# A three-layer interaction network on one core: low parts of four split groups on GpSimd, eleven split groups a phase, one fold for layers 0 and 1

## What is computed

```
def _L0_rec_ref(inputs, w0, w1, w2, b0, b1, b2):
    x0 = inputs
    xk = inputs
    ...
    for idx, (W, b) in enumerate(params):
        z = jnp.einsum('bhd,bkd,hks->bsd', x0, xk, W) + b[None, :, None]
        z = jax.nn.relu(z)
        if idx != n_layers - 1:
            half = z.shape[1] // 2
            xk = z[:, :half, :]
            direct.append(z[:, half:, :])
        else:
            direct.append(z)
    logit = jnp.sum(jnp.concatenate(direct, axis=1), axis=-1)
    return logit
e = jnp.stack([tbl_0[ids[:, 0]], tbl_1[ids[:, 1]], ...], axis=1)
z = _L0_rec_ref(e, L0_rec_w0, L0_rec_w1, L0_rec_w2, L0_rec_b0, L0_rec_b1, L0_rec_b2)
h = jnp.concatenate([z, dense_ctx], axis=1)
h = jnp.maximum(h @ W_top1 + b_top1, 0.0)
h = jnp.maximum(h @ W_top2 + b_top2, 0.0)
y = h @ W_top3
```

## Time and profile before

| | us |
|---|---|
| median of 3 runs | 697.9 (696.61 to 698.32) |
| the profiled execution | 697.3 |
| its span in the profile | 695.5 |
| mean granted TensorE clock | 0.975 of full speed |

### The profile page before, as it was taken

One profiled execution on the slowest core, in us unless ns is written; L12 is line 12 of the kernel. 1 busy time (PEld: TensorE's weight loads), 2 busy tenths in 40 slices (PEclk: granted clock), 3 DMA queues, 4 the chain that ended last, 5 costly groups with the idle time before them and its releaser, 6 DMA issues.

```text
span 695.5 us, 6053 instructions
## 1 busy us (share of the span) xinstructions
PE 640.6 (92%) x1856; PEld 349.2 (50%) x1856; DVE 600.8 (86%) x548; ACT 244.6 (35%) x315; POOL 361.4 (52%) x391
## 2 busy tenths in 40 slices
PE   0159789699999999999999999999999999999998
PEld 0025345355555555555555555555555555555544
DVE  0239679599999999999999999999999999999920
ACT  1112323343433434344334344343433443433312
POOL 6751573864747475766747574747475232232210
PEclk9978899899999999999999999999999999999999
DMA  9679953969493959586776949394958668170100
GB/s 210 125 201 282 304 121 80 321 157 328 82 310 85 283 154 254 180 213 221 164 275 125 318 99 332 76 308 101 285 151 228 204 147 282 65 237 1 62 0 0
DMA packets 126495, 128.14 MB, mean 184 GB/s; under 512 B 61407, under 2 KB 69359, under 8 KB 126464
## 3 DMA queue, kind: packets, MB, share of 16 engines
q1 hardware_dynamic: 117823, 126.25, 63.8%
q0 software_dynamic: 5120, 1.32, 2.0%
q10 hardware_dynamic: 3520, 0.20, 0.4%
HBM read 121.34 MB, written 6.39 MB: 184 GB/s over the span
## 4 chain that ended last, share of the span: by engine, by line
PE 80%; SPq 10%; issue 4%; DMA 3%; DVE 1%; ACT 0%; DVEq 0%; ACTq 0%
PE z L630 51%; PE z L620 8%; PE z L621 8%; PE z L622 8%; DMA rot<-fields 3%; SPq L266 3%; SPq L218 2%; SPq L220 1%; SPq L231 1%; SPq L216 1%; PE z L694 1%; PE z L638 1%; PE z L637 1%; PE top L684 1%; DVE whole L570 1%
## 5 line engine op out<-in xcount | busy, mean ns | idle before, releaser
L630 PE MATMUL z<-whole,w 128*128 128x512 f32 (+2 forms) x928 | 436.4, 604 | 16.7 <-DVE whole L570 16.0
L630 PEld LDWEIGHTS z<-whole,w 128*128 128x128 f32 (+2 forms) x928 | 178.4, 194 | 177.8 <-issue 157.7
L414 ACT ACTIVATE high<-raw 128x1024 fp32r<-128x1024 f32 (+1 forms) x128 | 135.3, 1058 | 328.1 <-DVE raw L562 288.3
L570 DVE TENSOR_TENSOR whole<-bc,xk 128x1024 f32<-128x1024 f32 (+1 forms) x208 | 230.0, 1131 | 18.2 <-ACT xk L425 9.8
L318 POOL DMA_INDIRECT emb<-in_tables,rows_all x160 | 195.9, 1225 | 54.4 <-issue 53.6
L546 DVE TENSOR_TENSOR low<-raw,high 128x1024 fp32r<-128x1024 f32 (+1 forms) x128 | 161.9, 1264 | 3.1 <-ACT high L414 3.1
L620 PE MATMUL z<-high,w_high 128*128 128x512 f32 (+1 forms) x256 | 140.9, 550 | 16.7 <-DVE low L546 16.7
L562 DVE TENSOR_TENSOR raw<-bc,xk 128x1024 f32<-128x1024 f32 x112 | 135.7, 1212 | 0.0
L336 POOL TENSOR_TENSOR stack<-stack_raw,stack 64x512 fp32r<-64x512 f32 x32 | 44.6, 1395 | 166.5 <-ACT stack L421 165.7
L621 PE MATMUL z<-high,w_low 128*128 128x512 f32 (+1 forms) x256 | 102.9, 402 | 0.0
L622 PE MATMUL z<-low,w_high 128*128 128x512 f32 (+1 forms) x256 | 102.8, 402 | 0.0
(11 more groups left out here) (52 smaller groups left out, 163.5 us busy)
## 6 DMA issues: line engine op xcount, KB each, us to landing
bc<-fields SPq DMA_DIRECT2D x64, 1024.0 KB, 9.2
rot<-fields SPq DMA_DIRECT2D x16, 1200.0 KB
bc<-fields SPq DMA_DIRECT2D x16, 768.0 KB
rot<-fields SPq DMA_DIRECT2D x16, 480.0 KB
fields<-xt SPq DMA_DIRECT2D x78, 64.0 KB
bc<-fields SPq DMA_DIRECT2D x32, 128.0 KB
rep<-fields SPq DMA_DIRECT2D x48, 80.0 KB
emb<-in_tables,rows_all POOLq DMA_INDIRECT x160
```

What stands on the lines that cost most here:

```text
L414: act.activation(high[0:m, k % PART_SLOTS], raw[0:m, k % RAW_SLOTS], ACT.Copy).then_inc(high_ready, 1)
L570: nc.vector.tensor_tensor(whole[0:rows, n % WHOLE_SLOTS, 0:len(tiles)], left, right, ALU.mult).then_inc(whole_ready, 1)
L630: ins = nc.tensor.matmul(z[layer][:, :], w[layer][0:m, WHOLE_AT[layer, t], :], whole[0:m, k % WHOLE_SLOTS, u], start=(t == 0), stop=(layer ...
```

## The change

- `SPLIT`: layer 1 splits groups 1, 3, 5, 7, 8 and layer 2 the same five; with layer 0's one, eleven groups a phase.
- In layer 2, from chunk 1 on, GpSimd makes the low parts of groups 1, 3, 5, 7 (`low_part` in its block), after the stack part of layer 1 and before that of layer 2. Group 8's, and all others, stay with VectorE. A semaphore `pool_low_ready` is waited for by TensorE before the group's matmuls and by VectorE before the raw slot is used again.
- `raw` has 3 slots, `high` 4, `low` 3. A low part waits until TensorE has done the split group three earlier.
- TensorE takes the split groups of layer 2 later: a group of GpSimd's 2.5 places and group 8 two places after its number (`order`).
- Layers 0 and 1 of a chunk are folded together on 128 rows (`fold01`), in the phase after the chunk's layer 1, right behind the gathers; `direct01` has two buffers for it.
- The transposed dense context is copied at the end of the loop, into a part of `bc[0]`; at the start ScalarE casts layer 0's split weights first.

```diff
...
@@ -39,12 +39,16 @@
 GT = 2
 G0 = -(-T0 // GT)
 G1 = T1 // GT
-SPLIT = {0: (1,), 1: (2, 4, 6, 8), 2: (2, 5, 8)}
+SPLIT = {0: (1,), 1: (1, 3, 5, 7, 8), 2: (1, 3, 5, 7, 8)}
+POOL_LOW = (1, 3, 5, 7)
 GROUPS = {0: G0, 1: G1, 2: G1}
 WHOLE_SLOTS = 4
-RAW_SLOTS = 2
-PART_SLOTS = 4
+RAW_SLOTS = 3
+HIGH_SLOTS = 4
+LOW_SLOTS = 3
 LAG = 2
+POOL_LAG = 2.5
 SECTION = 4
 SECTIONS = T1 // SECTION
 STORES = 3
...
@@ -63,6 +67,11 @@
 
 def split_tiles(layer):
     return [t for g in SPLIT[layer] for t in tiles_of(layer, g)]
+def by_pool(layer, c, g):
+    return layer == 2 and c > 0 and g in POOL_LOW
 
 
 def tower(nc, A, fields, out):
...
@@ -104,16 +113,16 @@
...
-        high = sb("high", [PART, PART_SLOTS, GT, N], fp32r)
-        low = sb("low", [PART, PART_SLOTS, GT, N], fp32r)
+        high = sb("high", [PART, HIGH_SLOTS, GT, N], fp32r)
+        low = sb("low", [PART, LOW_SLOTS, GT, N], fp32r)
...
-        direct = [sb("direct01", [PART, N]), sb("direct2", [PART, N])]
+        direct01 = [sb(f"direct01_{n}", [PART, N]) for n in range(2)]
+        direct2 = sb("direct2", [PART, N])
...
-        denseT = sb("denseT", [DENSE, BATCH])
...
+        denseT = bc[0][0:DENSE, 5, :]
...
@@ -193,8 +205,10 @@
...
-        FOLDED = [(0, 0), (1, 0), (0, 1), (0, 2), (1, 1)]
-        FOLDED += [x for p in range(1, CHUNKS + 1) for x in ((2, p - 1), (0, p + 2), (1, p + 1)) if x[1] in IN]
+        SPLITS = list(SPLIT_NO)
+        LOW_NO = {x: n for n, x in enumerate(x for x in SPLIT_NO if not by_pool(*x))}
+        POOL_LOW_NO = {x: n for n, x in enumerate(x for x in SPLIT_NO if by_pool(*x))}
+        FOLDED = [(1, 0)] + [x for p in range(1, CHUNKS + 1) for x in ((1, p), (2, p - 1)) if x[1] in IN]
...
@@ -219,6 +233,13 @@
...
+        def low_made(engine, layer, c, g):
+            x = layer, c, g
+            if by_pool(*x):
+                engine.wait_ge(pool_low_ready, POOL_LOW_NO[x] + 1)
+            else:
+                engine.wait_ge(low_ready, LOW_NO[x] + 1)
...
@@ -336,54 +359,64 @@
...
-            def fold(layer, c):
-                n = FOLDS * FOLD_NO[layer, c]
-                part = (slice(0, KEEP), slice(KEEP, PART), slice(0, PART))[layer]
-                column = layer // 2
-                src, width = direct[column], N // 2
+            def low_part(layer, c, g):
+                k = SPLIT_NO[layer, c, g]
...
-                pool.wait_ge(d_ready[layer], c + 1)
-                pool.tensor_tensor(halves[0][part, :], src[part, 0:width], src[part, width:2 * width], ALU.add).then_inc(d_free[layer], 1)
-                pool.wait_ge(d_free[layer], c + 1)
-                pool.tensor_tensor(halves[1][part, :], halves[0][part, 0:width // 2], halves[0][part, width // 2:width], ALU.add).then_inc(folded, 1)
-                pool.wait_ge(folded, n + 1)
-                pool.tensor_tensor(halves[2][part, :], halves[1][part, 0:width // 4], halves[1][part, width // 4:width // 2], ALU.add).then_inc(folded, 1)
-                pool.wait_ge(folded, n + 2)
-                pool.tensor_tensor(logits[part, column, c * SUB:(c + 1) * SUB], halves[2][part, 0:SUB], halves[2][part, SUB:2 * SUB], ALU.add).then_inc(folded, 1)
+                pool.wait_ge(high_ready, k + 1)
+                pool.wait_ge(parts_free, k + 1 - LOW_SLOTS)
+                pool.tensor_tensor(low[:, k % LOW_SLOTS], raw[:, k % RAW_SLOTS], high[:, k % HIGH_SLOTS], ALU.subtract).then_inc(pool_low_ready, 1)
+                issued["lows"] += 1
+            def summed(src, n, freed, count, dst):
+                width = N // 2
+                pool.tensor_tensor(halves[0][:, :], src[:, 0:width], src[:, width:2 * width], ALU.add).then_inc(freed, 1)
+                pool.wait_ge(freed, count)
+                pool.tensor_tensor(halves[1][:, :], halves[0][:, 0:width // 2], halves[0][:, width // 2:width], ALU.add).then_inc(folded, 1)
+                pool.wait_ge(folded, FOLDS * n + 1)
+                pool.tensor_tensor(halves[2][:, :], halves[1][:, 0:width // 4], halves[1][:, width // 4:width // 2], ALU.add).then_inc(folded, 1)
+                pool.wait_ge(folded, FOLDS * n + 2)
+                pool.tensor_tensor(dst, halves[2][:, 0:SUB], halves[2][:, SUB:2 * SUB], ALU.add).then_inc(folded, 1)
...
+            def fold01(c):
+                own_done()
+                pool.wait_ge(d_ready[0], c + 1)
+                pool.wait_ge(d_ready[1], c + 1)
+                summed(direct01[c % 2], FOLD_NO[1, c], d_free01, c + 1, logits[:, 0, c * SUB:(c + 1) * SUB])
+            def fold2(c):
+                own_done()
+                pool.wait_ge(d_ready[2], c + 1)
+                summed(direct2, FOLD_NO[2, c], d_free2, c + 1, logits[:, 1, c * SUB:(c + 1) * SUB])
...
-            fold(0, 0)
...
-            fold(1, 0)
-            fold(0, 1)
+            fold01(0)
...
-            fold(0, 2)
-            fold(1, 1)
...
-                fold(2, p - 1)
+                if p in IN:
+                    fold01(p)
+                fold2(p - 1)
...
-                if p + 2 in IN:
-                    fold(0, p + 2)
-                if p + 1 in IN:
-                    fold(1, p + 1)
...
+                    for g in POOL_LOW:
+                        low_part(2, p, g)
...
@@ -426,18 +459,18 @@
...
-                if c:
-                    act.wait_ge(d_free[0], c)
-                act.activation(direct[0][0:KEEP, :], z[0][KEEP:OUT, :], RELU, bias=bias[KEEP:OUT, 0:1]).then_inc(d_ready[0], 1)
+                if c > 1:
+                    act.wait_ge(d_free01, c - 1)
+                act.activation(direct01[c % 2][0:KEEP, :], z[0][KEEP:OUT, :], RELU, bias=bias[KEEP:OUT, 0:1]).then_inc(d_ready[0], 1)
...
-                if c:
-                    act.wait_ge(d_free[1], c)
-                act.activation(direct[0][KEEP:OUT, :], z[1][KEEP:OUT, :], RELU, bias=bias[KEEP:OUT, 1:2]).then_inc(d_ready[1], 1)
+                if c > 1:
+                    act.wait_ge(d_free01, c - 1)
+                act.activation(direct01[c % 2][KEEP:OUT, :], z[1][KEEP:OUT, :], RELU, bias=bias[KEEP:OUT, 1:2]).then_inc(d_ready[1], 1)
...
@@ -447,18 +480,16 @@
...
-                    act.wait_ge(d_free[2], c)
-                act.activation(direct[1][:, :], z[2][:, :], RELU, bias=bias[:, 2:3]).then_inc(d_ready[2], 1)
+                    act.wait_ge(d_free2, c)
+                act.activation(direct2[:, :], z[2][:, :], RELU, bias=bias[:, 2:3]).then_inc(d_ready[2], 1)
...
-            act.wait_ge(dense_t, 1)
-            act.activation(denseT[:, :], top[0][0:DENSE, :], ACT.Copy).then_inc(dense_ready, 1)
+            act.wait_ge(w0_ready, 2)
+            act.activation(w_high[0:ROWS0, 0:P0, :], to_split[0:ROWS0, 0:P0, :], ACT.Copy).then_inc(w_high_ready, 1)
...
-            act.wait_ge(w0_ready, 2)
-            act.activation(w_high[0:ROWS0, 0:P0, :], to_split[0:ROWS0, 0:P0, :], ACT.Copy).then_inc(w_high_ready, 1)
...
@@ -493,6 +524,11 @@
...
+                if p == CHUNKS:
+                    act.wait_ge(dense_t, 1)
+                    act.wait_ge(whole_ready, wholes_to(2, CHUNKS - 2, G1 - 1))
+                    act.wait_ge(raw_ready, splits_to(2, CHUNKS - 2, G1 - 1))
+                    act.activation(denseT, top[0][0:DENSE, :], ACT.Copy).then_inc(dense_ready, 1)
...
@@ -543,7 +579,9 @@
...
-                nc.vector.tensor_tensor(low[0:m, k % PART_SLOTS], raw[0:m, k % RAW_SLOTS], high[0:m, k % PART_SLOTS], ALU.subtract).then_inc(low_ready, 1)
+                if k >= LOW_SLOTS:
+                    dve.wait_ge(parts_free, k + 1 - LOW_SLOTS)
+                nc.vector.tensor_tensor(low[0:m, k % LOW_SLOTS], raw[0:m, k % RAW_SLOTS], high[0:m, k % HIGH_SLOTS], ALU.subtract).then_inc(low_ready, 1)
...
@@ -558,9 +596,10 @@
...
-                        dve.wait_ge(low_ready, k + 1 - RAW_SLOTS)
+                        low_made(dve, *SPLITS[k - RAW_SLOTS])
...
-                    pending.append([-1, (layer, c, g)])
+                    if not by_pool(layer, c, g):
+                        pending.append([-1, (layer, c, g)])
...
@@ -614,12 +653,12 @@
...
-                pe.wait_ge(low_ready, k + 1)
+                low_made(pe, layer, c, g)
...
@@ -637,12 +676,20 @@
...
+            def order(layer, c):
+                def place(g):
+                    if by_pool(layer, c, g):
+                        return g + POOL_LAG
+                    return g + LAG if layer == 2 and g in SPLIT[2] else g
+                return sorted(range(GROUPS[layer]), key=place)
...
-                for g in range(GROUPS[layer]):
+                for g in order(layer, c):
...
```

22 lines of the change are left out of this document (12 added, 10 removed).

## The result

The changed kernel takes **709.5 us** (median of four runs, 705.8 to 711.5) where the kernel before takes 698.1 (four runs on the same chip). The ratio is 1.0161, with a 95% interval of 1.0115 to 1.0207: slower by 1.6%. The profiled execution took 708.7 us, 706.9 of them its span, against 697.3 and 695.5 before. So 11.4 us have to be found.

What follows compares the result with a forecast made beforehand. TensorE and VectorE both nearly fill the 37.48 us period; blocking by GpSimd makes it 38.5. Ten periods +10, phases 12 and 13 +4.4, first phase +0.5, end -2: +12.9 on 697.3 gives 710.2 us, range 704 to 717 (8 in 10: 690 to 728).

Steps and rivals of the forecast that it cites:

- The mechanism: VectorE operations with two SBUF inputs and GpSimd tensor operations exclude each other for the whole instruction, and they alternate.
- The block of group 8's low part: End of layer 2: VectorE's low part waits for GpSimd's fourth low part, blocked 1.98 us a period.
- r: Start of VectorE's raw product of group 1 in layer 2; GpSimd's first low part was put at r + 2.35.
- The rotation product: VectorE's first rotation product stands behind GpSimd's stack operation after layer 2, blocked 1.28 us a period.
- The folds: GpSimd's two folds meet the last two low parts of layer 1, blocking VectorE 0.55 us a period.
- Run-up and first phase: Start to chunk 4's rotations: added low parts fall into waits for rotations, first phase +0.5 us.
- Phases 12 and 13: Without gathers, folds fall among rotation products: 1.75 us of blocking in place of 0.55, +2.2 each, +4.4.
- The last layer: Last layer and the top: -0.6 us, TensorE starting 4.6 us behind VectorE with 0.6 less to do.
- TensorE's idle time: TensorE idle 2 us a period ahead of split groups, released by VectorE's low part.
- the GpSimd-bound rival: GpSimd's low part takes 2.9 us, a period 3.0 longer, 733 us; stretched gathers do the same by smaller steps; chance 0.10.
- the even one: GpSimd just in time, folds meet nothing, blocking 1.28 + 1.28, period 37.4, 696 to 700 us; chance 0.12.
- "faster": Blocking costs less than read, under 1.6 us a period, so TensorE sets the pace: 684 us; chance 0.18.

Runs made afterwards that it cites:

- three low parts: Changed kernel with GpSimd making layer 2's low parts of groups 1, 3, 5 only and group 7's back on VectorE: 696.8 us, ratio 0.9998.
- The run with the old split groups: Changed kernel with split groups 2, 4, 6, 8 and 2, 5, 8 and no low part on GpSimd: 699.3 us, ratio 1.0027.
- The run with folds that wait: Changed kernel; folds in phases 12 to 14 wait for layer 1's first raw product, phase 15's stand behind low parts and stacked part: 704.8 us, ratio 1.0112.
- the half low parts: Changed kernel with GpSimd subtracting only the first of two tiles (128x512) in each of its four low parts: 686.2 us, ratio 0.983.
- The ten groups: Changed kernel with layer 2 splitting 1, 3, 5, 8 and GpSimd making the low parts of 1, 3, 5: 687.5 us, ratio 0.9864.
- 7 phases of one run: Changed kernel with all low parts on VectorE, none on GpSimd: 753.9 us, ratio 1.0828.

## Why the prediction was right, and where its steps were off

**The mechanism held.** VectorE's instructions with two SBUF inputs last until 1.08 or 1.09 us after the end of GpSimd's operation in the changed kernel (434.40 against 433.31), with three low parts (425.11 against 424.03), and are free where GpSimd's are short or done. The Trainium skill's rule of an exclusive lock for the whole instruction (SBUF — State Buffer, section "SBUF: two separate sides") is borne out by these rows.

**GpSimd's low part** was put at 2.4 us from three rows of other shapes. Unblocked ones take 2.35 to 2.40. The estimate of 2.25 from the Trainium skill (GPSIMD Engine Reference, section "Elementwise — side-by-side cycle accounting") was 6% low here.

**The block of group 8's low part** was to be 1.98 and is 2.36 in the period shown. Two small durations were mis-sized: from one low part to the next there are 0.22 us and not 0.1 (a cadence of 2.61, not 2.5), and the first starts at r + 2.55 (423.13 - 420.58) and not r + 2.35. Four pieces later GpSimd ends at r + 12.73 in place of r + 12.25. Against these 0.48, VectorE's instruction ends 1.08 us behind GpSimd's and not 1.21, for which the prediction made no allowance.

**The rotation product** was to lose 1.28 and lost 1.07. I had let VectorE's instruction wait for the whole of GpSimd's; but the stack operation started at 433.54, 0.78 us ahead of the product, and needed VectorE's low part to end first.

**The folds** were to block VectorE for 0.55 a period. In the steady period they block it for nothing; GpSimd is the one that waits, a 128x64 step at 1.42 us instead of 0.32 and a 128x256 step at 1.75 instead of 0.73. The price appears on GpSimd's side: it was to have 1.7 us to spare before its first low part, and has 0.38 (the folds take 6.28 us where 5.4 were put, and VectorE reaches r 23.2 us after GpSimd's stack operation ends and not 23.9). These three errors, +0.38, -0.21 and -0.55, make -0.4, and the period shown is 38.15 where 38.5 was put.

**GpSimd is not in time.** The ten periods run from 38.15 to 39.25, with a mean of 38.54, and the one shown is the shortest. It is the only one in which GpSimd's first low part waits for its cast. In the other nine it starts right behind the stack part of layer 1, at r + 2.6 to r + 3.6, so the 1.7 us to spare are used up. In the period with r = 343.00, GpSimd's first low part and VectorE's raw product of group 8:

```profile
346.56 2.39 POOL L367 TENSOR_TENSOR low<-raw,high 128x1024 fp32r<-128x1024 f32 x1
```

```profile
351.69 1.22 DVE L600 TENSOR_TENSOR raw<-bc,xk 128x1024 f32<-128x1024 f32 x1 [0.69 <-POOL low L367]
```

The block is 2.4 to 2.9 us in the ten periods, 2.6 in the mean, and in three of them VectorE also waits 0.15 to 0.69 for a raw slot, which the prediction had excluded: 34.65 + 2.6 + 0.1 + 1.1 = 38.5. This is read from the trace; no run isolates it. So the ten periods came to the forecast because two errors of 0.4 us a period cancel: the small terms above, and a GpSimd that is late. That part of the agreement is luck.

**Run-up and first phase** are the largest miss, -2.9 against +0.5. The assumption was that waits for rotations and for TensorE swallow what is saved. Of the 2.9 us, 1.8 are there already when the rest of chunk 3's rotations lands (129.11, now 127.34), and 1.2 are in the phase behind it (38.02 us, now 36.85). The 1.8 are no more than executions differ: five of the other kernels have the same instructions up to there, and their traces show 127.18, 127.56, 128.20, 128.77 and 129.41. In the phase behind it the wait of 2.82 for TensorE was one for a whole slot. VectorE of the changed kernel at the same place:

```profile
127.34 1.23 DVE L600 TENSOR_TENSOR raw<-rot,rep 120x1024 f32<-120x1024 f32 x1 [3.70 <-DMA rot<-fields]
...
134.18 1.22 DVE L609 TENSOR_TENSOR whole<-bc,xk 128x1024 f32<-128x1024 f32 x1 [0.41 <-DMA bc<-fields]
...
137.59 1.22 DVE L609 TENSOR_TENSOR whole<-bc,xk 128x1024 f32<-128x1024 f32 x1
```

The third whole group of layer 1 starts 10.25 us after the raw rotation product, as before (10.31), but since groups 1 and 3 are split now, a raw product and a low part more stand ahead of it: VectorE works where it waited. That is not the only way to these 1.2 us. The run with the old split groups has this phase at 36.91 us too, with a wait for TensorE of 1.74. TensorE's clock enters here: TensorE stands idle while the rotations are awaited, and the granted clock is 0.50 from 133 to 139 in the kernel before and from 130 to 136 in the changed one, and 0.50 for some 3 us only (134 to 137) with the old split groups. No run separates the two, and the cause of the 1.2 us stays open.

**Phases 12 and 13** cost 2.9 where 4.4 were put. The step was right in kind (folds among the rotation products) and too large: it put 1.75 of blocking in each phase, and the folds block 0.94 and 0.80. The run with folds that wait gets 4.1 us back and gives 1.4 to phase 14: phases 12 to 14 take 107.5 us there, 110.2 in the changed kernel and 108.2 in the kernel before.

**The last layer** was the step that had the wrong sign, +1.7 for -0.6. The prediction gave VectorE's and TensorE's saving and did not ask what stands ahead of the new low parts on GpSimd's and ScalarE's queues. VectorE and TensorE of the changed kernel in the last layer:

```profile
670.10 1.22 DVE L600 TENSOR_TENSOR raw<-bc,xk 128x1024 f32<-128x1024 f32 x1 [2.29 <-POOL low L367]
```

```profile
665.52 3.70 PE L669 MATMUL z<-whole,w 128*128 128x512 f32 x8 [0.78 <-ACT direct L484]
670.12 0.50 PE L659 MATMUL z<-high,w_high 128*128 128x512 f32 x1 [0.90 <-POOL low L367]
```

TensorE starts the layer 5.72 us behind VectorE, where it was 4.6: 1.1 us of the 1.7, since it has more of chunk 14 left. The other 0.6 is in the layer (16.6 us for 16.0), where the low parts come late.

**TensorE's idle time** was to be 2 us a period ahead of split groups, released by VectorE's low part. The window shows 0.78 (38.15 - 37.37), and 0.69 of it is ahead of layer 1's stack matmul at 422.80, released by GpSimd's stack part. The rest of the 1.85 between the period and the sum of 36.3 is hidden under matmuls whose ends are modelled: behind a whole group of four matmuls the next group starts 1.31 us after the group's own start where nothing is waited for (428.21 to 429.52), and 1.90 ahead of a split group at 414.98. The size was right; the place was right in part.

**The rivals.** Slots and semaphores fell with the half low parts; the GpSimd-bound rival had its low part at 2.9 us, and it is 2.4, but the smaller steps that this rival named are there in nine periods of ten, with up to 1.1 us; the even one had GpSimd nowhere behind and 1.28 us of block, where there are 2.36 and more; "faster" needed less than 1.6 us of blocking a period, and there are 3.4. The ten groups and the halves pass below that point and land at 687.5 and 686.2, near the 684 which that rival had for a period that TensorE sets.

## What to carry to other kernels

Work given to GpSimd costs VectorE the time that GpSimd's last operation overhangs into VectorE's next instruction with two SBUF inputs; so lay out when the last piece ends, gaps of 0.22 us included, and give GpSimd one piece less if it overhangs. Three pieces with ten split groups gained 1.4% here where four with eleven lost 1.6%. Look at every period and not at one: the shortest alone would have hidden that GpSimd was late in the other nine. For each new operation on a queue, ask also in the last rounds what stands ahead of it and who is asked for it there, since the steady period says nothing about the end.

## What the runs showed that was not expected

**Who gets the port pair next.** VectorE can keep GpSimd out through several instructions: 6.58 us for 1.3 us of work, in 7 phases of one run, while in other phases of the same run, and everywhere in the kernel before, GpSimd comes in after the first. In both cases GpSimd begins about 0.9 us after the start of a VectorE instruction of 1.21. In the seven, it comes in when VectorE has reached a product with `xk` from PSUM (420.61). What decides between the two is open; a wait on VectorE settles it for 1.17 us a period.

**TensorE's clock in the top product.** The eight matmuls that begin the top layers show 5.18 us in the changed kernel and 3.49 in the run with the edited end (TensorE of the two kernels, and a window around each; the number behind the busy time is the granted clock):

```profile
685.75 5.18 PE L729 MATMUL top<-logits,bc 128*128 128x480 f32 x8
...
685.00:695.00 10.00, 10.00 (x28) 0.83 0.00 0
```

```profile
681.11 3.49 PE L735 MATMUL top<-logits,bc 128*128 128x480 f32 x8
...
681.00:691.00 10.00, 10.00 (x37) 1.00 0.00 0
```

In the kernel before the same matmuls take 5.18 us too, and its windows of 1 us from 675 to 678 show a granted clock of 0.50 (1.2 GHz) with TensorE busy all through and for 20 us before. The edited end isn't the reason: of the ten traces, seven show the fall at this place, and three (three low parts, the old split groups, the edited end) do not. What decides it is open. So one execution in which the clock stays at full speed is 1.7 us shorter at this place, which is as much as some of the terms argued over above.
